# Cross-attention and routed experts on one core: a pipeline period with projections, reciprocals and work banks in another order

## What is computed

```python
q, k, v = (heads(layernorm(x), Wq, bq), heads(ctx, Wk, bk), heads(ctx, Wv, bv))   # 16 heads of 16
scores = einsum('bhqd,bhkd->bhqk', q, k) / 4        # 4 x 1024 queries, 77 keys, some masked
attn = einsum('bhqk,bhkd->bhqd', softmax(scores), v)
x = x + attn @ Wo.T + bo
t = layernorm(x)
idx, pmax = argmax and max of softmax(t @ Wr)        # 8 experts, at most 640 tokens each
x = x + where(kept, relu(t @ W1[idx]) @ W2[idx] * pmax, t)
```

## Time and profile before

| what | us |
|---|---|
| median of 3 runs (lowest, highest) | 554.75 (554.36, 555.15) |
| the profiled execution | 556.13 |
| its span, first to last instruction | 554.4 |
| TensorE matmuls busy | 466.1 (84%) |
| VectorE busy | 207.3 (37%) |
| ScalarE busy | 152.3 (27%) |
| GpSimd busy | 190.4 (34%) |
| mean granted clock of TensorE | 0.923 |

### The profile page before, as it was taken

The page is one execution under the profiler, slowest core; times in us unless marked ns, Lnnn a source line. Parts: engine busy times, 40 slices in busy tenths (PEclk is TensorE's granted clock), DMA queues, the critical chain, the costliest instruction groups (busy, mean ns, idle before and its releaser), DMA issues.

```text
span 554.4 us, 7679 instructions
## 1 busy us (share of the span) xinstructions
PE 466.1 (84%) x2823; PEld 313.5 (57%) x2823; DVE 207.3 (37%) x590; ACT 152.3 (27%) x224; POOL 190.4 (34%) x306
## 2 busy tenths in 40 slices
PE   5797869699999999968243399999999999999991
PEld 2342234253434343423132288999989989899891
DVE  5853336355656565544242123112131121313110
ACT  0145515535554646344101111101001010111000
POOL 4671603408585766060626202111101111221221
PEclk9999979889999999968575589999999999999997
DMA  6992633614232333333402406015060060624000
GB/s 202 321 273 93 192 95 91 201 45 143 83 134 96 123 109 106 119 106 120 148 0 80 145 1 214 28 44 187 19 204 29 20 218 20 214 95 145 6 30 0
DMA packets 51658, 62.35 MB, mean 112 GB/s; under 512 B 4658, under 2 KB 41561, under 8 KB 51616
## 3 DMA queue, kind: packets, MB, share of 16 engines
q1 hardware_dynamic: 46560, 53.53, 30.4%
q0 software_dynamic: 3456, 7.26, 3.7%
q10 hardware_dynamic: 1600, 1.01, 0.7%
HBM read 32.17 MB, written 27.41 MB: 107 GB/s over the span
## 4 chain that ended last, share of the span: by engine, by line
PE 67%; DMA 9%; DVE 8%; SPq 7%; issue 4%; POOL 3%; ACT 1%; ACTq 0%; POOLq 0%; DVEq 0%
PE tps L1317 11%; PE wk L1327 10%; PE tps L1337 10%; PE wk L1345 9%; PE wk L1185 6%; SPq L399 6%; PE wk L1097 5%; PE nat L1117 5%; DMA attn_mem<-rsum 4%; PE tps L1139 3%; PE wk L1169 3%; DMA strips<-shared 2%; DVE rowmax L807 2%; DVE attn_mem L836 2%; PE nat L1305 1%
## 5 line engine op out<-in xcount | busy, mean ns | idle before, releaser
L588 POOL DMA_INDIRECT out_x<-attn_mem,dest x40 | 39.0, 975 | 198.6 <-DVE attn_mem L1014 195.8
L623 ACT ACTIVATE shared<-tps,mask_key 77x1024 f32<-77x1024 f32 x64 | 67.5, 1104 | 28.9 <-PE tps L1143 28.9
L807 DVE TENSOR_REDUCE rowmax<-nat 128x8 f32<-128x616 f32 x58 | 46.3, 798 | 51.6 <-PE nat L1117 50.6
L1117 PE MATMUL nat<-kblk,qT 64*128 64x308 f32 x232 | 47.0, 481 | 16.5 <-DVE rowmax L807 16.5
L1317 PE MATMUL tps<-shared,w_sb 128*128 128x256 f32 x256 | 59.7, 393 | 0.6 <-ACT shared L679 0.6
L1327 PE MATMUL wk<-w_sb,shared 128*128 128x256 f32 x256 | 57.7, 379 | 0.0
L1337 PEld LDWEIGHTS tps<-shared,w_sb 128*128 128x128 f32 x480 | 56.0, 192 | 0.8
L1337 PE MATMUL tps<-shared,w_sb 128*128 128x128 f32 x480 | 56.0, 275 | 0.0
L1317 PEld LDWEIGHTS tps<-shared,w_sb 128*128 128x128 f32 x256 | 50.7, 198 | 8.4 <-issue 1.0
L1345 PE MATMUL wk<-w_sb,shared 128*128 128x256 f32 x240 | 54.3, 379 | 0.0
L1327 PEld LDWEIGHTS wk<-w_sb,shared 128*128 128x128 f32 x256 | 48.1, 190 | 6.3
(11 more groups left out here) (136 smaller groups left out, 522.8 us busy)
## 6 DMA issues: line engine op xcount, KB each, us to landing
w_sb<-in_w SPq DMA_DIRECT2D x16, 1024.0 KB, 8.4
strips<-shared SPq DMA_DIRECT2D x32, 256.0 KB, 3.7
slot_rows<-zeros SPq DMA_DIRECT2D x1, 5200.0 KB, 25.7
x_sb<-slot_rows SPq DMA_DIRECT2D x8, 650.0 KB
x_sb<-in_x SPq DMA_DIRECT2D x8, 512.0 KB, 8.9
attn_mem<-strips SPq DMA_DIRECT2D x32, 128.0 KB
attn_mem<-rsum SPq DMA_DIRECT2D x64, 64.0 KB
out_x<-base SPq DMA_DIRECT2D x8, 512.0 KB, 3.1
```

The source lines that it names most:

```text
L588: pool.indirect_dma_start(out_rows, bass.IndirectOffsetOnAxis(ap=dest[n % 2][:, c:c + 1], axis=0), y_sb[n % 2][:, c, :], None, bounds_chec ...
L623: act.activation(probsT[0:SK, r % 2, 2 * i:2 * i + 2, :], tps[0:SK, 2 * i:2 * i + 2, :], ACT.Exp, bias=mask_key[:, g // GPB:g // GPB + 1]) ...
L807: dve.tensor_reduce(rowmax[:, j, :, m, :], nat_heads(g, k), AX.X, ALU.max).then_inc(rowmax_ready, 1)
L1117: last = pe.matmul(dst, qT[g % 2][of, m, j * P:(j + 1) * P], kblk[of, b, m, :, :].rearrange("p (i r) k -> p i (r k)", i=2), start=True, st ...
```

## The change

- `sums` and `rsum` are 32 rows of 256 instead of 64 of 128; a gather writes 8 rows; `spread` issues four transfers of twice the size instead of eight.
- TensorE: `project(r, 0)` stands between `scores(c, 1)` with `natural_scores` 2 and `weigh_values` 1; `router_logits` and `project(r, 1)` follow `natural_scores` 4; `transpose_logits` follows `scores(c, 3)`; the two halves of `transpose_xn` stand on either side of `count_before` and `natural_scores` 7. Round 1 instead of round 2 uses `wk[1]`, and the waits on the banks' readers follow.
- VectorE: `invert_sums` comes first, ahead of `second_norm` and row maximum 0; `normalise_attn` follows row maximum 1, the residuals follow 2 and 4, `choose` follows 5, `masked_positions` 6. Without a c, `choose` comes ahead of `normalise_attn`.
- ScalarE: `copy_attn` waits for the gathers of the group before (`sums_loaded`) instead of `rsum_ready`; the copy of the logits and the exponential of `choose` come one round later.

```diff
@@ -144,8 +144,8 @@
         maxT = sb("maxT", [P, GT], BF16)
         shared = sb("shared", [P, 2 * 4 * GT + ROUNDS * GT])
         attn_mem = sb("attn_mem", [P, 3, KD, GT])
-        sums = sb("sums", [HALF, P])
-        rsum = sb("rsum", [HALF, P])
+        sums = sb("sums", [QUARTER, 2 * P])
...
         V_LOADS = 2
-        SPREADS = 16 * KD * TPG
+        SPREADS = 16 * KD * 2
 
...
                     wait(sp, rsum_ready, g)
-                sp.dma_start(sums[16 * r:16 * (r + 1), :], attnU[DH:P:QUARTER, r, :].rearrange("p (t n) -> p t n", t=TPG)
+                sp.dma_start(sums[8 * r:8 * (r + 1), :], attnU[DH:P:QUARTER, r, :].rearrange("p (t n) -> p t n", t=2)
                              ).then_inc(sums_loaded, 16)
 
...
                 for m in range(KD):
-                    for t in range(TPG):
-                        sp.dma_start(recip[:, m, t * P:(t + 1) * P],
-                                     rsum[m * 32 + t:m * 32 + 32:TPG, None, :].broadcast_to([HH, DH, P])
+                    for t in range(2):
+                        sp.dma_start(recip[:, m, t * 2 * P:(t + 1) * 2 * P],
+                                     rsum[m * 16 + t:m * 16 + 16:2, None, :].broadcast_to([HH, DH, 2 * P])
                                      ).then_inc(recip_spread, 16)
 
...
                 wait(act, strip_stored[r], 16 * g)
-                wait(act, rsum_ready, g)
-                act.copy(attnU[:, r, :], wk[1 if r == 2 else 0][:, :]).then_inc(attnU_ready, 1)
+                wait(act, sums_loaded, 16 * ROUNDS * g)
+                act.copy(attnU[:, r, :], wk[1 if r == 1 else 0][:, :]).then_inc(attnU_ready, 1)
 
...
@@ -648,18 +648,17 @@
                     copy_tT(o)
                 if has(c):
                     exponentials(c, 1)
+                    copy_attn(c, 1)
+                    exponentials(c, 2)
                 if has(o):
                     wait(act, lgT_ps, o + 1)
                     act.copy(lgT[:, :], wk[1][:, 0:P]).then_inc(lgT_ready, 1)
                 if has(c):
-                    copy_attn(c, 1)
-                    exponentials(c, 2)
+                    copy_attn(c, 2)
+                    exponentials(c, 3)
                 if has(o):
                     wait(act, lsh_ready, o + 1)
                     act.activation(lexp[:, :, :], lsh[:, :, :], ACT.Exp).then_inc(lexp_ready, 1)
-                if has(c):
-                    copy_attn(c, 2)
-                    exponentials(c, 3)
                 if has(a):
                     copy_xnT(a)
                 if has(c):
...
                     prepare_mask()
+                if has(r):
+                    invert_sums(r)
                 if has(o):
                     second_norm(o)
                 if has(n):
                     row_maxima(n, 0)
-                if has(r):
-                    invert_sums(r)
-                if has(n):
                     row_maxima(n, 1)
                 if a == 1:
                     first_norm(1)
+                if not has(c) and has(o):
+                    choose(o)
+                if has(r):
+                    normalise_attn(r)
                 if has(n):
                     row_maxima(n, 2)
                 if has(r):
-                    normalise_attn(r)
+                    add_residual(r, 0)
                 if has(n):
                     row_maxima(n, 3)
-                if has(o):
-                    choose(o)
-                if has(n):
                     row_maxima(n, 4)
                 if has(r):
-                    add_residual(r, 0)
+                    add_residual(r, 1)
                 if has(n):
                     row_maxima(n, 5)
+                if has(c) and has(o):
+                    choose(o)
+                if has(n):
                     row_maxima(n, 6)
-                if has(r):
-                    add_residual(r, 1)
-                if has(n):
-                    row_maxima(n, 7)
                 if has(o):
                     masked_positions(o)
                 if has(n):
+                    row_maxima(n, 7)
                     split_maxima(n)
                 if n == 0:
                     bias_values(2)
...
@@ -1144,26 +1140,28 @@
                     if q % 2:
                         last.then_inc(scoresT_ps, 1)
 
-            def weigh_values(g, r, a, o):
+            def weigh_values(g, r, a, n, rr, o):
                 m, par = r // 2, r % 2
                 if r == 0:
                     wait(pe, v_ready, B if g // GPB > 1 else B // 2)
                     wait(pe, attnU_ready, ROUNDS * g)
                 if r == 1:
                     if has(o):
-                        wait(pe, tT_ready, KD * (o + 1))
-                    wait(pe, attnU_ready, ROUNDS * g + 1)
+                        wait(pe, tT_ready, KD * o + 1)
+                    else:
+                        wait(pe, q_ready, KD * n + KD)
                 if r == 2:
-                    if has(o):
-                        wait(pe, lsh_ready, o + 1)
+                    if has(rr):
+                        wait(pe, x1_ready, 2 * rr + 2)
+                    else:
+                        wait(pe, attnU_ready, ROUNDS * g + 1)
                 if r == 3:
                     if has(a):
                         wait(pe, xnT_ready, KD * a + 1)
-                    elif g > 0:
-                        wait(pe, x1_ready, 2 * g)
-                    wait(pe, attnU_ready, ROUNDS * g + 2)
+                    else:
+                        wait(pe, attnU_ready, ROUNDS * g + 3)
                 wait(pe, probsT_ready, 2 * (ROUNDS * g + r) + 2)
-                bank = wk[1 if r == 2 else 0]
+                bank = wk[1 if r == 1 else 0]
                 for q in range(4):
                     h = m * HH + 2 * q + par
                     last = pe.matmul(bank[q * QUARTER:(q + 1) * QUARTER, :], v_ones[:, g // GPB, h, :], probsT[0:SK, r % 2, q, :],
...
                     wait(pe, attn_ready, KD * (g + 1))
-                    if has(c):
-                        wait(pe, attnU_ready, ROUNDS * c + 2)
-                    elif has(o):
+                    if has(o):
                         wait(pe, tT_ready, KD * (o + 1))
+                    elif has(c):
+                        wait(pe, attnU_ready, ROUNDS * c + 1)
                 else:
                     wait(pe, x1_ready, 2 * g + 1)
                 for j in range(2):
...
@@ -1204,9 +1200,11 @@
                         last = pe.transpose(wk[1 - k][:, j * P:(j + 1) * P], t_sb[:, j, k * P:(k + 1) * P], ident[:, :])
                     last.then_inc(tT_ps, 1)
 
-            def router_logits(g):
+            def router_logits(g, c):
 
                 wait(pe, tT_ready, KD * (g + 1))
+                if has(c):
+                    wait(pe, attnU_ready, ROUNDS * c + 2)
                 for k in range(KD):
                     for j in range(TPG):
                         last = pe.matmul(wk[1][j * QUARTER:(j + 1) * QUARTER, 0:P], wr_sb[:, k, :], tT[:, k, j * P:(j + 1) * P],
...
                 if has(o):
-                    transpose_t(o, n, c, r)
+                    transpose_t(o, n, c)
                 if has(c):
                     scores(c, 1)
+                elif has(o):
+                    router_logits(o, c)
+                    transpose_logits(o)
                 if has(n):
                     natural_scores(n, 2)
-                if has(o):
-                    router_logits(o)
-                if has(c):
-                    weigh_values(c, 1, a, o)
-                if has(n):
-                    natural_scores(n, 3)
-                if has(c):
-                    scores(c, 2)
-                if has(o):
-                    transpose_logits(o)
-                if has(n):
-                    natural_scores(n, 4)
                 if has(r):
                     if r == 0:
                         pe.wait_ge(w_attn_loaded, 16 * ATTN_W_LOADS)
                     project(r, 0, c, o)
+                if has(c):
+                    weigh_values(c, 1, a, n, r, o)
+                if has(n):
+                    natural_scores(n, 3)
+                if has(c):
+                    scores(c, 2)
+                if has(n):
+                    natural_scores(n, 4)
+                if has(c) and has(o):
+                    router_logits(o, c)
+                if has(r):
+                    project(r, 1, c, o)
                 if has(n):
                     natural_scores(n, 5)
                 if has(c):
-                    weigh_values(c, 2, a, o)
+                    weigh_values(c, 2, a, n, r, o)
                     scores(c, 3)
+                    if has(o):
+                        transpose_logits(o)
                 if has(n):
                     natural_scores(n, 6)
-                if has(r):
-                    project(r, 1, c, o)
+                if has(a):
+                    transpose_xn(a, 0, c, o)
```

58 lines of the change are left out of this document (26 added, 32 removed).

## The result

The changed kernel takes **588.2 us** (586.96 to 588.42, 4 runs) beside 554.95 us for the kernel before (554.36 to 555.57, 4 runs): ratio 1.059, interval 1.0575 to 1.0613. The forecast was 564.5 us with a range of 553.5 to 570. The sign was right; the loss is 33 us where 10 were predicted.

What follows compares the result with a forecast made beforehand. TensorE was taken as the bound in steady periods, VectorE with little slack. Terms 1.5 + 2.9 + 3.0 + 0.9 + 1.7 gave +10.0 us on 556.13, or 566.1; for the median 564.5 us, range 553.5 to 570.

Steps and rivals of the forecast that it cites:

- The reciprocal: VectorE's reciprocal of the sums, now 256 elements a partition: grows from 936 ns to 1.73 us, taken as 1.75.
- The rival of 0.94 us: VectorE's reciprocal keeps its old length, the loop is 28.5 us and the kernel 560.5 us; chance 0.14.
- The estimate from the Trainium skill: VectorE's reciprocal as iterated divide: 128 more elements cost 1.07 us instead of 0.80, the sum some 1.3 us larger.
- The loop of VectorE and TensorE: Steady periods: 29.3 us instead of 28.3, two old waits replaced by some 2 us before `natural_scores` 1; +3.0 in all.
- The spreads' landing: SP's four spreads per group: landing covered by row maxima 0 and 1, costed at nothing; -0.3 us behind the weights.
- the rival of the early spread: SP's queue, periods 1 and 2: spreads don't wait for weights, landing about 4.7 us after first issue; 549.7 us, chance 0.14.
- 0.5 us thin: Steady periods: the cover of the spreads' landing by row maxima 0 and 1 is short by about this; not costed.
- clock falls in the steady periods too: TensorE's gap of about 2 us lowers its clock, about 2 us a fall, two or three falls: 569 to 571; chance 0.14.
- Period 1 and 2: Projection 0 moved ahead leaves work behind it where spreads land late, at 72.6 and 108.0: +1.5 and +2.9 us.
- The drain: Behind the last group, reciprocal and `choose` come before normalising: sums' landing to projection 0 takes 11.5 us, was 9.8; +1.7.

Runs made afterwards that it cites:

- e8: Changed kernel with a tile's sums on every second partition, so a spread reads rows at a distance of 4: 570.2 us, ratio 1.029.
- e16: Changed kernel with a tile's sums on every third partition, so a spread reads rows at a distance of 6: 577.9 us, ratio 1.041.
- e11: Changed kernel with a tile's sums on every fourth partition, so a spread reads rows at a distance of 8: 581.3 us, ratio 1.040.
- e1: Changed kernel's order with the old 64 x 128 sums and eight spreads: 575.9 us, ratio 1.035.
- e3: Changed kernel without GpSimd's indirect transfers of rows to their slots, only the pipeline compared: 567.2 us, ratio 1.013.
- e4: Changed kernel with projection 0 moved behind `natural_scores` 4 and the normalising behind row maximum 3: 570.2 us, ratio 1.023.
- e5: Changed kernel with projection 0 behind `natural_scores` 4, normalising behind row maximum 3, 64 x 128 sums and eight spreads: 570.0 us, ratio 1.024.
- e10: Kernel before the change with the normalising moved behind row maximum 3 on VectorE: 547.3 us, ratio 0.987.

## Why the prediction was wrong

- **The reciprocal** (1.73 us predicted by the slope): 1.71 to 1.74. Right, and the same with 64, 96 or 128 partitions (e8, e16, e11). The rival of 0.94 us is out. The estimate from the Trainium skill (VectorE: DVE Perf Modes, "First, the fixed hardware budget"), 936 ns and 1.07 us more, some 2.0 us, does not come out either: the measurement decides.
- **The loop of VectorE and TensorE** (29.3 us, 2 us before `natural_scores` 1): close where the landing allows it. In e8 periods 3 and 4 take 29.9 and 29.4 us, with 1.23 us before `natural_scores` 1 and 1.18 before projection 0 in period 4; period 5 takes 31.2, the clock falling behind a wait of 1.69 us before `natural_scores` 1. The two old waits went, and 0.37 before `natural_scores` 7 came, as said.
- **The spreads' landing**: this step failed. I wrote that "the longer rows move at about that pace" (168 GB/s), "since a spread still reads 8 rows as before", that the landing is covered by row maxima 0 and 1, and costed it at nothing. Two things were wrong in it. First the length: a spread still reads 8 rows, but they lie on four ports instead of eight. The group's packets run from 170.4 to 176.8 us, in e8 from 165.0 to 168.8; the four issues take 3.45 us, in e8 2.67, about the 2.6 that I had said; and the landing takes 8.13 us, not the 4.7 that the rival of the early spread put on it. Second the cover: the spreads don't "start 4 to 5 us earlier relative to the projection", they have less time. Before, TensorE was ready for projection 0 8.9 us after the first issue (159.16 to 168.07, without its wait of 0.72); now it is ready after 5.8 (169.12 to 174.92, and 5.8 in e1 and e8 too). Landing and normalising of the first half must fit into that: 8.13 + 1.35 leave a wait of 3.68, the 6.84 of e1 2.67, and even the 5.63 of e8 leaves 1.18. With "0.5 us thin" I had named the place but not priced its failing.
- **What this triggers**: 3.7 to 4.3 us of waiting before projection 0 in each of periods 3 to 6, and the clock falls behind it (projection 2.7 to 3.8 us instead of 1.99). The rival "clock falls in the steady periods too" had the second half of this with 2 us a fall; it lacked the first, and put the fall at the gap before `natural_scores` 1, where it came in e3 and in one period of e8. From `natural_scores` 1 to 7 it was 22.6 us instead of 17.6, and the rest of the loop 0.8 shorter: 29.3 + 5.0 - 0.8 = 33.5.
- **Period 1 and 2** (+1.5, +2.9): +1.9 and +1.9; period 3 starts at 130.7 instead of the predicted 129.6, 1.8 of it from start-up. The landing came at 74.47 and 109.32 (72.6 and 108.0 predicted), with the start-up's 1.8 us in the first. The rival in which the spread doesn't wait for the weights is out.
- **The drain** (+1.7): from the sums' landing to projection 0, 298.97 to 310.05 = 11.1 us (11.5 predicted, 9.8 before). But most of the +4.2 lies earlier, in period 7, which the sum left at nothing. From its first `scores` to value product 3 it takes 28.1 us instead of 23.9, for the same reason as the steady ones: TensorE waits 4.32 us before projection 0, where it did not wait before, and then runs it at half clock (before, then after):

```profile
254.07 1.99 PE L1185 MATMUL wk<-wo_sb,attn_mem 128*128 128x256 f32 x8
...
280.44 3.78 PE L1183 MATMUL wk<-wo_sb,attn_mem 128*128 128x256 f32 x8 [4.32 <-DVE attn_mem L835]
```

  The way from there to the next projection 0 is 1.3 us shorter, and the one behind it 1.3 longer; projection 1 took 3.78 instead of 1.99 us there.

So of the 33 us some 17 are the ports. With the rows on eight ports (e8) the loss is 2.9%, some 16 us: the end of the range, and more than the +10 of the sum. In e8's profile the start-up and period 1 together cost +3.0 us (+3.6 after the change), period 2 and periods 3 to 6 +1.5, +1.6, +1.1, +2.9 and -0.2, close to the sum's terms; period 7 with the drain costs +5.9 where I had 1.7. Part of that is a wait of 2.35 us before projection 0 in period 7 and TensorE at half clock; it was not taken apart further. That placing the projection elsewhere doesn't rescue the rest of the order is shown by e4 and e5; whether an order with ScalarE's exponentials earlier would, was not tried.

## What to carry to other kernels

When a small tile is repacked into fewer partitions, count not how many rows each transfer reads but how many different fours of partitions, taken within each 32, they lie in (below and above partition 64 apart): 8 rows on 2, 4 and 8 of them gave 49, 95 and 193 GB/s. Fewer and larger transfers bring the landing forward only while that count stays: 5.63 us in e8 and 8.13 after the change, where it had been 6.74. Before an engine's step is moved ahead, measure from the first issue to the moment at which the engine is ready to use the data, and hold the landing against it. And a wait that is "about covered" should be priced as if its cover were gone: here it was the largest term. Taking the waiting step one place later on VectorE gave 1.3% in the kernel before, about a third of it by way of the clock.

## Unexpected on the hardware

- A broadcast read from 8 partitions is bound by the partitions' ports as soon as two of them share one: 46 ns for 1,024 bytes alone on a port, about 80 (up to 88) with two rows, 142 to 166 with four. For 512 bytes it is 27 and 37 to 47 ns.
- Moving rows farther apart can make it slower again: a distance of 4 partitions 46 ns, of 8 about 80.
- The length of TensorE's wait alone doesn't tell whether the clock falls: behind 3.68 to 4.34 us the projection was slow each time (2.72 to 3.78 us), but in e11 it took 1.99 us behind 3.38 us and 3.13 behind 1.67, in e10 1.99 behind 1.69.
